# Attention step of a four-layer graph network: one run of the weighted values per head group, and spread sums turned by transposes

## What is computed

```python
scores = jnp.einsum('bhqd,bhkd->bhqk', q, k) * SCALE
scores = scores * (adj + adj)[:, None, :, :]
attn = jax.nn.softmax(scores, axis=-1)
ctx = jnp.einsum('bhqk,bhkd->bhqd', attn, v)
x = x + (ctx heads side by side) @ Wo.T + bo
```

## Time and profile before

| | |
|---|---|
| three timed runs | 3280.47, 3283.55, 3296.8 us |
| the profiled execution's own time | 3286.39 us |
| its span, first to last instruction | 3284.6 us |
| busy share PE, PE weight loads, DVE, ACT, POOL | 95%, 74%, 60%, 47%, 22% |
| mean granted TensorE clock | 0.981 of full |
| a batch | about 411 us |
| its attention loop with W (batch 2) | 550 to 682 us |

### The profile page before, as it was taken

How to read it: one execution, slowest core, us unless ns; L and a number is a source line. 1 busy time by engine, 2 the same in 40 slices (tenths; PEclk the granted TensorE clock), 3 DMA queues, 4 the chain that set the end, 5 groups by cost and what they waited for, 6 DMA issues and landing times.

```text
span 3284.6 us, 64796 instructions
## 1 busy us (share of the span) xinstructions
PE 3133.9 (95%) x23624; PEld 2445.3 (74%) x23624; DVE 1956.5 (60%) x4281; ACT 1527.9 (47%) x2801; POOL 728.1 (22%) x1241
## 2 busy tenths in 40 slices
PE   6899998999989999899998999989999899999999
PEld 5677786777867778677786786767867678677886
DVE  2588426884268843687436874368743786437863
ACT  1485225842258431683326832268322673227722
POOL 0144002440024300243002430024200242003420
PEclk8999999999999999999999999999999999999999
DMA  3301203012030120301203012030111201112000
GB/s 111 78 2 34 74 14 78 2 33 74 14 78 2 33 75 14 78 2 33 74 14 78 2 33 74 16 76 2 39 69 27 65 11 43 55 39 53 24 11 13
DMA packets 75097, 135.39 MB, mean 41 GB/s; under 512 B 8592, under 2 KB 43792, under 8 KB 74768
## 3 DMA queue, kind: packets, MB, share of 16 engines
q1 hardware_dynamic: 74768, 131.01, 14.2%
HBM read 72.26 MB, written 8.39 MB: 25 GB/s over the span
## 4 chain that ended last, share of the span: by engine, by line
PE 78%; SPq 7%; DVE 5%; issue 4%; ACT 3%; DMA 1%; POOL 1%; DVEq 0%; ACTq 0%; POOLq 0%
PE ps L1006 35%; PE ps L1211 14%; PE ps L1147 13%; PE ps L1173 8%; SPq L425 7%; PE ps L1127 5%; PE ps L1055 1%; ACT Z L934 1%; DVE stats L574 1%; POOL rstd L484 1%; PE ps L1155 1%; DVE hT L608 1%; DMA qS<-qlo 1%; ACT h2T L960 0%; PE ps L1038 0%
## 5 line engine op out<-in xcount | busy, mean ns | idle before, releaser
L739 DVE CUSTOM_DVE_ANT_0 Z<-ps,adjN 128x1024 f32<-128x1024 f32 x512 | 621.5, 1215 | 108.2 <-PE ps L1127 108.1
L1147 PE MATMUL ps<-ident,Z 128*128 128x128 f32 x4096 | 570.5, 283 | 70.9 <-ACT PT L924 39.9
L1147 PEld LDWEIGHTS ps<-ident,Z 128*128 128x128 f32 x4096 | 464.7, 144 | 194.8 <-issue 93.5
L934 ACT ACTIVATE Z<-Z,nm 128x1024 f32<-128x1024 f32 x512 | 587.8, 1148 | 33.6 <-POOL nm L493 29.5
L924 ACT ACTIVATE PT<-ps 128x512 f32<-128x512 f32 x592 | 342.2, 592 | 157.7 <-PE ps L1147 100.8
L1127 PE MATMUL ps<-kS,qS 128*128 128x512 f32 x1024 | 378.4, 454 | 6.8 <-ACT qS L914 6.8
L694 DVE COPY PT<-ps 128x512 f32<-128x512 f32 x432 | 297.5, 689 | 139.6 <-PE ps L1147 104.7
L482 POOL TENSOR_SCALAR ve<-mv 128x4 f32<-128x4 f32 x80 | 15.8, 197 | 1433.8 <-DVE mv L579 1433.1
L505 POOL TENSOR_SCALAR H<-adjN 128x128 fp32r<-128x128 f32 (+1 forms) x456 | 317.4, 696 | 0.0
L1173 PEld LDWEIGHTS ps<-PT,v 128*32 128x32 f32 x8192 | 214.6, 111 | 99.6 <-issue 74.1
L1173 PE MATMUL ps<-PT,v 128*32 128x128 f32 x8192 | 281.5, 280 | 6.4
(11 more groups left out here) (166 smaller groups left out, 5292.0 us busy)
## 6 DMA issues: line engine op xcount, KB each, us to landing
adjN<-adj_in SPq DMA_DIRECT2D x8, 4096.0 KB, 17.0
kS<-khi SPq DMA_DIRECT2D x48, 256.0 KB, 3.9
kS<-klo SPq DMA_DIRECT2D x48, 256.0 KB, 5.1
qS<-qhi SPq DMA_DIRECT2D x96, 128.0 KB, 3.0
qS<-qlo SPq DMA_DIRECT2D x96, 128.0 KB, 3.0
xn<-x_in SPq DMA_DIRECT2D x8, 1024.0 KB, 6.5
out<-x SPq DMA_DIRECT2D x8, 1024.0 KB, 4.8
W1h<-w1T SPq DMA_DIRECT2D x9, 512.0 KB, 5.7
```

The source lines that it names most:

```text
L739: dve.tensor_tensor_reduce(Z[:, u % ZS], ps[:, 2 * (u % 2):2 * (u % 2) + 2].rearrange("p a n -> p (a n)"), adjN[:, u // HEADS], SCORE_SCAL ...
L934: act.activation(Z[:, u % ZS], Z[:, u % ZS], ACT.Exp, bias=nm[:, u:u + 1], accum_out=sm[:, u:u + 1]).then_inc(exps.sem, 1)
L1147: mm = pe.transpose(ps[:, turn_bank((u, s)), rows(a)], Z[:, u % ZS, rows(NT // 2 * s + a)], ident[:])
```

## The change

The weighted values of a group are issued in one run of 64 instructions in step 4g + 6, and nothing in step 4g + 7, so `pv_ps` rises in step 4g + 6. The two products with the identity in `spread_inverses` become two transposes, two instructions in place of four.

```diff
@@ -295,7 +295,7 @@
         INVERT, SPREAD, COPY, WEIGH, NORMALISE, PROJECT, ADD = 4, 5, 6, 6, 9, 10, 11
-        PARTS = (NT // 2, NT // 2)
+        PARTS = (NT,)
         STEPS = UNITS + HEADS + 2
@@ -1152,8 +1152,8 @@
                     for g in range(GROUPS):
-                        mm = pe.matmul(ps[:, at, first + P * g:first + P * (g + 1)],
-                                       rs[:, HPG * g:HPG * (g + 1)].rearrange("p h d -> p (h d)"), ident[:], start=True, stop=True)
+                        mm = pe.transpose(ps[:, at, first + P * g:first + P * (g + 1)],
+                                          rs[:, HPG * g:HPG * (g + 1)].rearrange("p h d -> p (h d)"), ident[:])
                     mm.then_inc(R_ps.sem, 1)
```

## The result

The changed kernel takes 3327.55 us (median of 4 runs, 3324.91 to 3332.45) against 3285.2 us: ratio 1.0125, 95% interval 1.0095 to 1.0155. It is **42 us slower**. The forecast was 12 us slower, with a range up to 3332 us, which holds the value.

A forecast was written before the change was run, and what follows sets the result against it. PE was taken to set the pace, with three plain steps after merging exposing a unit's 3.84 us way from S to T: 52 x 0.28 = +14.6 us, -2.3 at the loop's end, together +12, 3296 us; range 3240 to 3332.

The forecast's parts named there:

- PE's work: Merging W on PE: two W steps of 2.50 us become 3.37 and 1.34, -0.29 us per group.
- Rival 1: Buffers cover the three plain steps and PE stays the bound: tile 16.17 us, -1.13, time 3222 us; chance 0.20.
- The transposes: Sp, with two instructions fewer, gets 0.22 us shorter per tile, and the saving reaches W in full.
- S of unit 5 to S of unit 9: From r = 3 to r = 7: T 3.84 us after S, O then waits for DVE's copy; 9.18 us.
- S of unit 9 to S of unit 13: From r = 7 to the next r = 3: T at 3.84 us, Sp 0.88 later, W 0.95 after that; 8.40 us.
- other late ones: Search for further delays: DVE's and ACT's copies in the long W step were judged to be on time.
- The loop's end: No scores are left to be late, so PE's -0.29 us comes through once per batch: -2.3 us.
- The sum: 52 tiles at +0.28 us give +14.6 us, with -2.3 at the loop's end: together +12 us, 3296 us.
- the likeliest case: The forecast itself: tile 17.58 us, time 3296 us, own range 3288 to 3304 us; chance 0.55.
- rival 2: DVE's pace of 1.75 us per unit bounds the plain steps: +0.97 us per tile, time 3332 us; chance 0.12.
- Rival 3: Turning `rs` by transposes takes what the products took: tile 17.80 us, time 3307 us; chance 0.10.
- Rival 4: Idle PE lowers the clock once per tile, costing 0.86 us each time: +58 us, time 3342 us; chance 0.03.

The follow-up runs named there:

- e1: The merging of W alone, products with the identity kept, against the kernel before: 3345.4 us, ratio 1.0173.
- e2: The transposes alone, W in two halves as before, against the kernel before: 3269.88 us, ratio 0.9947.
- e3: The changed kernel with POOL's filler of step r = 0 issued in r = 2: 3302.87 us, ratio to before 1.0042.
- e4: The changed kernel with DVE's reciprocal issued before the copy of unit u - 2 in r = 0: 3295.15 us, ratio to before 1.0023.

## Why the prediction was right, and what it missed

The direction and the mechanism were right: with the merging, T waits for a unit's way around the other engines, and that costs more than PE saves. The size was not: 12 us were forecast and 42 measured.

**PE's work.** Right. W to T went from 1.01 or 1.02 to 1.89, which is 0.87 more, and a W step's other 1.16 us went, so each part that is cut off costs PE 0.29 us. Rival 1, which counts only this, is refuted by the idle time before T.

**The transposes.** Right to 0.01 us per tile, by e1 against the change and e2 against before. A transpose instruction costs 0.11 us like one of a product's two. It is not four times faster, as the Trainium skill, TensorE: Matmul & The Clock Gate, section Terms, has it for FP32; by that figure the tile would have fallen by an estimated 0.33 us, and it fell by 0.23.

**S of unit 5 to S of unit 9.** 9.18 forecast; 9.17, 9.16 and 8.93 in three tiles, mean 9.09. T at 3.84 was 3.85. The wait of O for DVE was real in two tiles of three, as said, but smaller: T to O is 1.05 there and 0.92 in the third, a wait of 0.13 where the sum has 5.00 - 4.72 = 0.28.

**S of unit 9 to S of unit 13. This step failed in size:** 8.40 forecast, 8.95 measured (633.22 to 642.17). The prediction took the way of the earlier trace rows, a stretch without spreading and filler, and wrote "T at 3.84" for r = 1. In r = 0 POOL has both between two maxima, and they start only when DVE's reciprocal is through, which is queued behind the copy of unit 6. 4.35 - 3.84 = 0.51 of the 0.55 is this; e3 and e4 took 0.47 and 0.48 back. The rest is T to Sp, 0.92 for 0.88. The delay could have been read beforehand, from 1.97 us between Z and exponential in r = 1 of the kernel before. My list of other late ones had DVE's and ACT's copies, not what stands behind them, nor POOL.

**The loop's end. Wrong in sign:** -0.29 forecast, +0.56 measured (8.38 to 8.94). With the whole W before it the last but one T comes 2.84 us after O (683.18 to 686.02) instead of 1.97 (673.38 to 675.35), and copy, reciprocal, spreading and Sp are queued behind it. DVE and POOL in the changed kernel, then in the kernel before:

```profile
686.02 2.00 PE L1147 MATMUL ps<-ident,Z 128*128 128x128 f32 x16
...
687.15 0.69 DVE L694 COPY PT<-ps 128x512 f32<-128x512 f32 x1 [1.55 <-PE ps L1147]
...
687.76 0.19 DVE L699 RECIPROCAL sm<-sm 128x8 f32<-128x8 f32 x1
...
688.17 0.86 POOL L500 TENSOR_SCALAR rs<-sm 128x256 f32<-128x256 f32 x1 [2.07 <-DVE sm L699]
...
689.08 0.44 PE L1155 MATMUL ps<-ident,rs 128*128 128x128 f32 x2 [1.06 <-POOL rs L500]
```

```profile
677.09 0.19 DVE L699 RECIPROCAL sm<-sm 128x8 f32<-128x8 f32 x1
...
678.41 0.71 PE L1155 MATMUL ps<-ident,rs 128*128 128x128 f32 x4
```

Copy, reciprocal and spreading end in a PE idle for 1.06 us at Sp, where PE did not wait before. So the last W starts 6.27 us after O instead of 5.88, which is 0.39 of the 0.56. e4 shows it: 8.33 with the reciprocal first. The other 0.17 lies between the last W and O (2.67 for 2.50), and its cause was not looked for.

**The sum.** Per batch 4.40 us over six tiles and 0.56 at the end; times eight 39.7 of the 42. The forecast of 3296 lay 32 too low; the likeliest case's own range, 3288 to 3304, did not hold the value, the wide one did. That is luck: the wide range reached to 3332 for the sake of rival 2, whose mechanism is refuted, and not for a way that is half a microsecond longer in r = 1. What the forecast comes close to is e4, the change without POOL's delay: a tile of 17.55 for 17.58, and 3295 us for 3296.

**The rivals.** Rival 2 named 3332 us, and the time came near it, but not by its mechanism: it wanted every T at 4.2 us and no idle DVE, while T of r = 5 came at 3.85 and DVE's copy in its step r = 4 had waited 1.66 us for its transposes:

```profile
624.57 0.69 DVE L694 COPY PT<-ps 128x512 f32<-128x512 f32 x1 [1.66 <-PE ps L1147]
```

The Trainium skill, TensorEngine Tiling (Array Packing), section PSUM Bottleneck, says that the copies out of PSUM may become the bound. Here they did not: this copy waited for PE. Rival 3 is refuted by e2. Rival 4 is refuted too: PE idled twice a tile, for 0.95 us in r = 1 and up to 0.46 in r = 5, and the granted clock over six tiles was 1.00. (By its own sum it would have cost 57 us, not 58.)

## What to carry to other kernels

When engine time is spread evenly between hand-over points, it can hide the way of one item around the other engines; before work is bunched, compare the longest stretch without it to that way, step by step, since fillers and once-per-tile instructions make the way longer in some steps than in others. Take the way from a step that has them, even if it is covered there, and follow what is queued *behind* each instruction that comes later, across engines (copy, reciprocal, spreading, maximum, exponential). Added work that costs nothing in one version and its full price in the other is a quick test of which engine is really waited for.

## What was not expected of the hardware

A float32 transpose of 128 columns took 0.11 us per instruction in a run, the same as each half of a float32 product, so turning `rs` with it saved just half. Twelve idle gaps of PE before T in 108 us of the changed kernel, from 0.19 to 0.95 us long, did not lower the granted clock from 1.00.
